# Key bias moved from a TensorE product to a VectorE addition, merged steps and weight chunks in another order

## What is computed

```python
q, k, v = heads(x@Wq + bq), heads(x@Wk + bk), heads(x@Wv + bv)   # 16 heads of 16
q = elu(q) + 1;  k = elu(k) + 1
k = k / sqrt(sum(k*k, -1) + 1e-6)
a = (q @ k.T) @ v                      # = q @ (k.T @ v), as the kernel does it
y = layernorm(x + a@Wo + bo, 1e-6) * gamma + beta
x1 = layernorm(x + y)
g, u = fp4(x1) @ fp4(w_gate).T, fp4(x1) @ fp4(w_up).T
out = layernorm(x1 + fp4(silu(g)*u) @ fp4(w_down).T)
```

## Time and profile before

| | |
|---|---|
| median of three runs | 726.67 us |
| the profiled execution | 728.29 us, span 726.6 us |
| PE busy | 694.5 us, 96% of the span |
| DVE, ACT, POOL busy | 81%, 67%, 85% |

### The profile page before, as it was taken

How to read it: one execution, slowest core, us unless ns; L and a number is a source line. 1 busy time by engine, 2 the same in 40 slices (tenths; PEclk the granted TensorE clock), 3 DMA queues, 4 the chain that set the end, 5 groups by cost and what they waited for, 6 DMA issues and landing times.

```text
span 726.6 us, 13704 instructions
## 1 busy us (share of the span) xinstructions
PE 694.5 (96%) x4114; PEld 617.0 (85%) x4114; DVE 590.5 (81%) x1436; ACT 484.3 (67%) x943; POOL 616.6 (85%) x955
## 2 busy tenths in 40 slices
PE   7899999999886899999999999999999999999995
PEld 5788888887765789999999999999999999999995
DVE  4687888865566789989899898998989989898874
ACT  4567666764556567676776777767777677677664
POOL 3698889887888699988898888988889888899766
PEclk9899999999999999999999999999999999999998
DMA  8333433334321011112111121111211112100001
GB/s 284 111 131 132 134 132 131 131 132 162 128 88 59 30 59 46 44 46 71 45 59 45 45 74 44 59 45 45 73 44 60 45 45 74 45 30 16 16 31 43
DMA packets 22269, 55.01 MB, mean 76 GB/s; under 512 B 2546, under 2 KB 5556, under 8 KB 22196
## 3 DMA queue, kind: packets, MB, share of 16 engines
q1 hardware_dynamic: 21776, 54.01, 21.8%
q10 hardware_dynamic: 420, 0.13, 0.1%
HBM read 28.90 MB, written 25.17 MB: 74 GB/s over the span
## 4 chain that ended last, share of the span: by engine, by line
PE 84%; POOL 7%; issue 4%; DVE 2%; DMA 1%; SPq 1%; ACT 1%; POOLq 0%; DVEq 0%
PE banks L361 21%; PE banks L363 21%; PE banks L362 20%; PE banks L492 7%; PE banks L467 6%; PE banks L397 3%; POOL arena L1009 2%; PE banks L372 2%; DMA resid<-in_L_ffn_w_up_dram 1%; PE banks L506 1%; PE banks L505 1%; PE banks L424 1%; PE banks L385 1%; POOL lnbuf L1056 1%; POOL arena L1071 1%
## 5 line engine op out<-in xcount | busy, mean ns | idle before, releaser
L361 PE MATMUL banks<-wgu_hi,actT_lo 128*128 128x512 f32 (+1 forms) x384 | 150.4, 392 | 2.6 <-DVE actT_lo L871 1.9
L362 PE MATMUL banks<-wgu_lo,actT_hi 128*128 128x512 f32 (+1 forms) x384 | 144.3, 376 | 0.0
L363 PE MATMUL banks<-wgu_hi,actT_hi 128*128 128x512 f32 (+1 forms) x384 | 143.6, 374 | 0.0
L659 ACT ACTIVATE arena<-banks 128x512 f32<-128x512 f32 x64 | 38.4, 600 | 115.7 <-PE banks L363 115.6
L1071 POOL TENSOR_TENSOR arena<-arena 128x960 f32<-128x960 f16 (+2 forms) x68 | 115.2, 1694 | 0.0
L1047 POOL TENSOR_TENSOR arena<-arena 128x704 f32<-128x704 f32 x64 | 89.2, 1394 | 20.2 <-DVE arena L858 18.3
L361 PE MATMUL banks<-wd_hi,actT_lo 128*128 128x256 f32 x320 | 100.1, 313 | 0.0
L871 DVE TENSOR_TENSOR actT_lo<-banks,actT_hi 128x512 fp32r<-128x512 f32 (+1 forms) x132 | 85.4, 673 | 17.5 <-ACT actT_hi L645 16.9
L363 PE MATMUL banks<-wd_hi,actT_hi 128*128 128x256 f32 x320 | 90.3, 282 | 0.0
L362 PE MATMUL banks<-wd_lo,actT_hi 128*128 128x256 f32 x320 | 90.2, 282 | 0.0
L361 PEld LDWEIGHTS banks<-wgu_hi,actT_lo 128*128 128x128 f32 x384 | 72.7, 189 | 12.3 <-DVE actT_lo L871 2.8
(11 more groups left out here) (125 smaller groups left out, 1961.7 us busy)
## 6 DMA issues: line engine op xcount, KB each, us to landing
xs<-x_plus_scratch SPq DMA_DIRECT2D x32, 512.0 KB, 3.2
x_plus_scratch<-xs SPq DMA_DIRECT2D x24, 512.0 KB, 2.9
arena<-in_L_attn_x_dram SPq DMA_DIRECT2D x32, 256.0 KB, 3.5
out_dram<-arena SPq DMA_DIRECT2D x32, 256.0 KB, 2.1
x_plus_scratch<-arena SPq DMA_DIRECT2D x8, 512.0 KB, 2.9
resid<-in_L_ffn_w_down_dram SPq DMA_DIRECT2D x1, 704.0 KB, 7.5
resid<-in_L_ffn_w_gate_dram SPq DMA_DIRECT2D x1, 640.0 KB, 8.3
resid<-in_L_ffn_w_up_dram SPq DMA_DIRECT2D x1, 640.0 KB, 9.6
```

The source lines that it names most:

```text
L361: nc.tensor.matmul(dst, sl, mh, start=(k == 0), stop=False, skip_group_check=shared)
L362: nc.tensor.matmul(dst, sh, ml, start=False, stop=False, skip_group_check=shared)
L363: last = nc.tensor.matmul(dst, sh, mh, start=False, stop=(ended and k == n - 1), skip_group_check=shared)
```

## The change

Three things. (1) The product with `rows` in `kv_project` is gone, with the small operations that prepared `rows`. `bk` is now broadcast to all 128 partitions by its DMA, 1 is added once (L804), and a new DVE operation `k_bias` adds it while it moves the keys from the bank to SBUF (tile `kb`, the words of `ksq`). `k_exps` and `k_features` read `kb` instead of the bank. PE waits for `k_lin` instead of `k_feat` before it writes the bank again. (2) Chunks of weights start in iterations 2, 4, ..., 18, 19, 20 instead of 0, 2, ..., 20. (3) The `first` of ACT and DVE is cut in two: the keys' part (`first_keys`) comes after `step`. POOL takes `roots` first, then the keys' root and scaling, then the rest of `step`, then `x_biases` (`first_loads`). `attend` of the first eight tiles alternates between two banks. The core of the diff:

```diff
...
@@ -218,10 +217,11 @@
                 cols = [DW + i * D + k * P for i in range(i0, i1)]
                 WG.append((cols, wgu_hi[:, k, i0 * P:i1 * P], wgu_lo[:, k, i0 * P:i1 * P]))
-        PACE = 2
+        CHUNK_STEP = [2, 4, 6, 8, 10, 12, 14, 16, 18, 19, 20]
+        assert len(CHUNK_STEP) == NCH
         WG_STEP = {}
         for g, (cols, _, _) in enumerate(WG):
-            ready = PACE * ((max(cols) + P - 1) // CW) + 4
+            ready = CHUNK_STEP[(max(cols) + P - 1) // CW] + 4
             WG_STEP[max([ready] + [step + 1 for step in WG_STEP])] = g
         def wg_view(g):
@@ -267,7 +267,11 @@
             return Q_BANK if b < B - 1 else KV_BANK + 1
         def at_bank(u):
-            return T_BANK + 1 if u < 10 else AT_BANK
+            return T_BANK + u % 2 if u < 8 else T_BANK + 1 if u < 10 else AT_BANK
+
+        def at_read(u):
+
+            return u - 1 if u < 8 else u
         def aggregated(t):
@@ -375,15 +379,13 @@
             def kv_project(p):
                 pe.wait_ge(xT_lo_s, p + 1)
-                after(pe, k_feat, kv_read(p))
+                after(pe, k_lin, kv_read(p))
                 after(pe, v_s, kv_read(p))
                 for jj in range(2):
                     bank = kv_banks(p) + jj
                     c = slice((p % PPB) * 2 * P + jj * P, (p % PPB) * 2 * P + (jj + 1) * P)
-                    split_product(ps[:, bank, :], lambda k: (xT_hi[:, k, c], xT_lo[:, k, c]),
-                                  lambda k: (wkv_hi[:, k, :], wkv_lo[:, k, :]), KT, ended=False, shared=True)
-                    last = nc.tensor.matmul(ps[:, bank, 0:D], rows[:, D:], rows[:, 0:D], start=False, stop=True,
-                                            skip_group_check=True)
+                    last = split_product(ps[:, bank, :], lambda k: (xT_hi[:, k, c], xT_lo[:, k, c]),
+                                         lambda k: (wkv_hi[:, k, :], wkv_lo[:, k, :]), KT)
                 last.then_inc(kv_ps, 1)
             def kv_accumulate(p):
@@ -459,9 +460,9 @@
             def attend(u):
                 pe.wait_ge(mo_sb, u // TPB + 1)
                 pe.wait_ge(q_feat, 2 * (u // 4) + 2)
-                after(pe, y1_s, u)
+                after(pe, y1_s, at_read(u))
                 if u == 0:
-                    pe.wait_ge(k_feat, MERGE)
+                    pe.wait_ge(k_lin, MERGE)
                     pe.wait_ge(v_s, MERGE)
                 for m in range(KT):
                     last = nc.tensor.matmul(ps[:, at_bank(u), 0:D], resid[:, u, m * P:(m + 1) * P], mo[:, u // TPB, m, :],
@@ -486,11 +487,13 @@
             def turn(n):
                 c0, c1 = chunks(n)
+                if n == 0:
+                    pe.wait_ge(y1_s, 7)
                 pe.wait_ge(deq_s, n + 1)
                 after(pe, vT_lo_s, n)
                 for c in range(c0, c1):
                     last = nc.tensor.transpose(ps[:, T_BANK + c // 4, (c % 4) * P:(c % 4 + 1) * P],
-                                               va[:, n % 2, c * P:(c + 1) * P], ident[:, :])
+                                               va[:, (n + 1) % 2, c * P:(c + 1) * P], ident[:, :])
                 last.then_inc(vT_ps, 1)
             def down(t):
@@ -575,10 +578,9 @@
                 nc.scalar.activation(qe, qr, ACT.Exp, scale=-1.0).then_inc(q_e, 1)
             def k_exps(p):
-                act.wait_ge(kv_ps, p + 1)
+                act.wait_ge(k_lin, p + 1)
                 after(act, k_feat, p)
-                b = kv_banks(p)
-                nc.scalar.activation(kexp, ps[:, b:b + 2, 0:D], ACT.Exp, bias=mone[:, :]).then_inc(k_exp, 1)
+                nc.scalar.activation(kexp, kb, ACT.Exp, bias=mone[:, :]).then_inc(k_exp, 1)
             def k_squares(p):
                 act.wait_ge(k_feat, p + 1)
@@ -615,6 +615,8 @@
                     q_maps(p - 2)
                 if p == NP + 1:
                     nc.scalar.preload_act_table_set("silu_and_others")
+
+            def first_keys(p):
                 if pair(p):
                     k_exps(p)
                 if p in WG_STEP:
@@ -701,6 +703,7 @@
                 first(p)
                 if p >= MERGE:
                     step(FIRST + p - MERGE)
+                first_keys(p)
             for t in range(FIRST + TAIL, LAST + 2):
                 step(t)
@@ -766,9 +767,17 @@
             def k_features(p):
                 dve.wait_ge(k_exp, p + 1)
                 after(dve, k_hat, p - 1)
+                nc.vector.scalar_tensor_tensor(out=kf[:, p % 2, :].rearrange("p (j c) -> p j c", j=2), in0=kexp, scalar=1.0,
+                                               in1=kb, op0=ALU.min, op1=ALU.max).then_inc(k_feat, 1)
+
+            def k_bias(p):
+                if p == 0:
+                    dve.wait_ge(bk_one_s, 1)
+                dve.wait_ge(kv_ps, p + 1)
+                after(dve, k_ssq, p)
                 b = kv_banks(p)
-                nc.vector.scalar_tensor_tensor(out=kf[:, p % 2, :].rearrange("p (j c) -> p j c", j=2), in0=kexp, scalar=1.0,
-                                               in1=ps[:, b:b + 2, 0:D], op0=ALU.min, op1=ALU.max).then_inc(k_feat, 1)
+                nc.vector.tensor_tensor(kb, ps[:, b:b + 2, 0:D], bk_one[:, :].unsqueeze(1).broadcast_to([P, 2, D]),
+                                        ALU.add).then_inc(k_lin, 1)
             def v_bias(p):
                 after(dve, kv_acc, p - 2)
@@ -791,13 +800,8 @@
             def first(p):
                 if p == -1:
-                    dve.wait_ge(rows_hi_s, 1)
-                    dve.wait_ge(rows_zero, 1)
-                    nc.vector.tensor_tensor(rows[0:2, 0:D], rows_st[:, 0:D], f32(rows_hi[:, 0:D]),
-                                            ALU.subtract).then_inc(rows_lo_s, 1)
-                    nc.vector.tensor_copy(rows[0:2, D:], f32(rows_hi[:, D:])).then_inc(rows_s, 1)
-                    dve.wait_ge(rows_lo_s, 1)
-                    nc.vector.tensor_copy(rows[0:1, 0:D], f32(rows_hi[0:1, 0:D])).then_inc(rows_s, 1)
+                    dve.wait_ge(bk_in, 16)
+                    nc.vector.tensor_scalar(bk_one[:, :], bk_one[:, :], 1.0, None, ALU.add).then_inc(bk_one_s, 1)
                 if pair(p + 1):
                     x_low(p + 1)
                 if p == -1:
@@ -818,9 +822,12 @@
                     mask_heads((p - 6) // PPB)
                 if pair(p - 2):
                     q_features(p - 2)
+
+            def first_keys(p):
                 if pair(p):
+                    k_bias(p)
+                    v_bias(p)
                     k_features(p)
-                    v_bias(p)
                 if p in WG_STEP:
                     weights_low(WG_STEP[p])
                 if pair(p):
@@ -936,13 +943,11 @@
                 if joint(t + 4):
                     joint_scales(t + 4)
-            dve.wait_ge(rows_in, 16)
-            dve.wait_ge(small_set, 4)
-            nc.vector.tensor_scalar(rows_st[:, 0:D], rows_st[:, 0:D], 1.0, None, ALU.add).then_inc(rows_st_s, 1)
             for p in range(-1, MERGE + TAIL):
                 first(p)
                 if p >= MERGE:
                     step(FIRST + p - MERGE)
+                first_keys(p)
             for t in range(FIRST + TAIL, LAST + 1):
                 step(t)
@@ -1013,6 +1018,8 @@
                 if pair(p - 1):
                     k_newton(p - 1)
                     k_normalise(p - 1)
+
+            def first_loads(p):
                 if p == 0:
                     pool.wait_ge(xb_in, 2 * 16)
                 if pair(p):
@@ -1084,10 +1091,14 @@
                     dequantise(t + 2)
             for p in range(-1, MERGE + TAIL):
+                if p >= MERGE:
+                    roots(FIRST + p - MERGE)
                 first(p)
                 if p >= MERGE:
                     step(FIRST + p - MERGE)
+                first_loads(p)
             for t in range(FIRST + TAIL, LAST + 2):
+                roots(t)
                 step(t)
...
```

More of the change, by code:

```diff
@@ L73, in build @@
         headmask = sb("headmask", [P, P])
-        rows = sb("rows", [P, D + P], F32R)
+        bk_one = sb("bk_one", [P, D])
         gamma_b = sb("gamma_b", [P, D])
@@ L235, in chunk_at @@
         def chunk_at(step):
-            return step // PACE if step % PACE == 0 and 0 <= step // PACE < NCH else None
+            return CHUNK_STEP.index(step) if step in CHUNK_STEP else None
         def there(t):
@@ L594, in first @@
                 if p == -1:
-                    act.wait_ge(rows_st_s, 1)
-                    nc.scalar.activation(rows_hi[:, :], rows_st, ACT.Copy).then_inc(rows_hi_s, 1)
+                    act.wait_ge(small_set, 3)
                 if pair(p + 1):
@@ L1025, in roots @@
             def roots(t):
+                if t < FIRST + 2:
+                    return
                 s = t % 2
@@ L1076, in step @@
                     pool.wait_ge(late_in, 2 * 16)
-                if t > FIRST + 1:
-                    roots(t)
                 if joint(t + 3):
```

29 lines of the change are left out of this document (12 added, 17 removed).

## The result

The changed kernel takes 740.68 us (median of four runs, 739.32 to 741.09), the kernel before 727.46 beside it (four runs, 725.34 to 728.38): a ratio of 1.018 with an interval from 1.016 to 1.020. It is slower. The prediction was 733.3 with a range of 717 to 743: the sign of its likeliest case is right, but +6.6 us stands against a measured +13.2 (+12.2 in the span), and the time lies above the 728 to 740 that this case had for itself.

What follows compares the result with a forecast made beforehand. PE bounded the pair stretch before; a loop over DVE and ACT was to bound it after, POOL still the merged stretch. +8.6 - 1.0 - 1.0 = +6.6 on 728.29 gave 734.9, less 1.6 for the median: 733.3 us, range 717 to 743.

Steps and rivals of the forecast that it cites:

- likeliest case: Whole kernel: slower by 6.6 us, 733.3 us, with its own range from 728 to 740; chance 0.45.
- The start: Before the pair stretch: `k_bias` of pair 0 at 12.3, about 4.2 us gained on the keys' path, less 0.3 for `bk`.
- The moved chunks: Pair stretch: chunks bunched at 18, 19, 20 but the same in number, so they cost nothing, at most 1 us.
- The loop without blocking: Pair stretch: the links over DVE and ACT, with `mask_heads` in one iteration of four, sum to 6.31 us a pair.
- The product on PE is worth nothing once DVE's loop decides: Pair stretch: removing the bias product saves 5.0 us only if PE stays the bound; PE waits instead, so that gain goes.
- DVE near 19: Sign in the windows from 40 to 140: DVE busy near 19 of 20, with PE about 17.5.
- Blocking, 0.36 per pair: Pair stretch: `k_features` with two SBUF inputs contends with POOL, a mean wait of 0.36 us a pair, loop 6.67.
- The merged stretch and its end, -1.0 and -1.0: Merged stretch: POOL's wait goes but blocking takes time, -1.0 us; PE's waits at the end, -1.0 us more.
- The first, nobody blocked: Rival: `k_features` doesn't block POOL; pair stretch +0.3, merged stretch -4.5, end -1, in all 721.5 us; chance 0.27.
- The second, PE stays the bound: Rival: DVE's loop stays under 5.91 us a pair and PE bounds the pair stretch, -17.8, 709 us; chance 0.08.
- The third, 0.9 per pair: Rival: the wait is a whole POOL operation or hits twice, 0.9 instead of 0.36 a pair, 746 us; chance 0.12.
- The fourth: Rival: pair stretch as forecast, but the end of the merged stretch gives back 5 us, 728.5 us; chance 0.08.

Runs made afterwards that it cites:

- e3: The kernel after, but `k_features` takes its second input from the bank instead of SBUF (bias left out of that branch): 731.73 us, ratio 1.008.
- e12: The kernel before with only the chunks of weights moved to start from pair 2: 723.64 us, ratio 0.996.
- e7: The kernel before with only the new order of the merged steps and the second bank of `attend`: 723.11 us, ratio 0.996.
- e2: The kernel before with only the key bias moved to DVE, chunks and order as before: 751.89 us, ratio 1.036.
- e6: The kernel after, but the broadcast of `bk` is issued by SP after the first two tiles of `x`, `Wk` and `Wv`: 739.1 us, ratio 1.017.

## Why the prediction was half right

The steps that failed are three terms of the sum, all too small. The start: `k_bias` of pair 0 was put at 12.3, right after the preparations on DVE, as if these ended where they had before. The moved chunks: put at "nothing, at most 1". The loop without blocking: put at 6.31. They measured 14.39, 2.1 (between F(22) and F(24)) and 6.45. One by one:

- **The product on PE is worth nothing once DVE's loop decides:** right. PE is down to 16.1 to 18.8 of 20, and DVE and ACT are the ones waited for. The sign "DVE near 19" was wrong: DVE is at 16.1 to 17.1 from 60 to 160. Neither engine of this loop gets full.
- **The loop of 6.31 without blocking:** measured 6.45 (e3). The exp out of SBUF took 0.72 to 0.73 us where I had taken 0.63 from L575, which reads SBUF too but adds no tile. From `k_bias` to `k_features` it is 1.48 (125.76 to 127.24), not 1.39. The two waits inside it (0.19 and 0.70) are where the prediction had them.
- **Blocking, 0.36 per pair:** measured 0.32. With the loop, 6.67 was forecast and 6.77 came. The second half of the mechanism showed as well, in the 3.01 of POOL's L1014. That the size came out is partly luck: it was worked out for arrivals at random, but the two operations meet in nearly every pair. POOL loses about 0.45 each time, DVE 0.15 or less in 14 of 19 pairs, and three pairs carry over half of DVE's loss.
- **The bunched chunks, "nothing, at most 1":** failed. e12 against e7 puts 2.1 us on F(22) to F(24) with PE as the bound, and with the bias on DVE these two pairs take 15.49, where two average ones take 13.54: 1.9 to 2.1 either way. Taken over F(3) to F(24), the moved chunks cost 1.4 with the bias on PE (e12 against e7: 130.2 and 128.8) and 2.4 with it on DVE (the kernel after against e2: 144.1 and 141.7). I had counted the chunks and not when they come. How much the bunching does, and how much that all eleven chunks now lie behind F(2), stays open: no run starts them late without three neighbours.
- **The start, 4.2 gained less 0.3:** failed in size. Only 1.8 came. F(2) was to be at 24.1 and was at 26.16: the first `x` was 2 us late and `k_bias` of pair 0 began at 14.39, not 12.3. From there to F(2) it took 11.8, near the forecast 11.5. DVE's timeline:

```profile
10.87 0.69 DVE L727 TENSOR_TENSOR actT_lo<-banks,actT_hi 128x512 fp32r<-128x512 f32 x1 [0.76 <-ACT actT_hi L550]
11.48 1.75 DVE L814 TENSOR_TENSOR wq_lo<-resid,wq_hi 128x512 fp32r<-128x512 f32 x1
...
14.39 0.68 DVE L779 TENSOR_TENSOR arena<-banks,bk_one 128x512 f32<-128x512 f32 x1
```

  The second `x_low` began 1.8 later than before (9.05 there), and `wq_lo`, with two inputs in SBUF beside POOL, took 1.75 instead of 1.38. The load of `bk`, which the prediction gave 0.3, makes the first tile later by 1.1 to 2.3 us in six traces, and by 0.3 to 0.8 when it is issued later (e6); in e6 F(2) moved by 0.6 only, so the rest of the late start stays open.
- **The merged stretch and its end, -1.0 and -1.0:** right in the sum, -1.7, but by luck: two misses cancel. POOL's period fell to 8.17 (forecast 8.39), while PE's longest wait grew from 3.84:

```profile
244.56 2.05 PE L468 MATMUL banks<-mo,resid 128*128 128x256 f32 x4 [8.41 <-DVE lnbuf L901]
```

  Blocking hid more than half of what the order gives: without it (e3) the stretch gains 5.5 instead of 1.7.

Summed at F(24), +13.9 came where +8.6 was forecast. The 5.3 too little: 2.1 at the start, 19 pairs of 6.77 instead of the 6.69 that the prediction's sum gives (147.1 over 22), 1.6, the bunching, 15.49 - 13.38 = 2.1, less 0.5 that F(2) to F(3) came shorter. The mechanism was right, and the sizes of its start, of its chunks and, a little, of its loop were not.

**The rivals.** The first, nobody blocked, had 721.5. Blocking was real, and even with it taken away the time is 731.7: the price of that rival was 10 us too low. Its 5.5 for all behind F(24) came exactly (97.67 against 103.20); what it missed lies ahead, where F(24) was to be +0.3 and is +7.6 in e3. The second, PE stays the bound, is false. The third, 0.9 per pair, is false in the mean but true of single pairs (1.75 and 1.81 us for a `k_features`). The fourth, that the end of the merged stretch wins back 5 because PE's waits there go, is false: the longest of them grew to 8.41.

## What to carry to other kernels

An operation added to an engine with idle time can still cost as much as its own length (here 0.68 us a pair for one of 0.68), if it stands on a chain that goes back and forth between two engines: add up the links of that loop, waits included, and put instructions into the waits that don't depend on it. Where the result moves from a PSUM bank to SBUF, look at what the reader's inputs become, and whether POOL is reading SBUF at that moment. And time each part of a bundle of edits apart: here two of three helped by 8 us, and the bundle lost 13.
